# Attention's batch loops written out on five engines, and the last batch's outputs loaded first in the mixer

## What is computed

```python
x = x + _L0_xattn_ref(_layernorm(x), ctx_1024, Wq, bq, Wk, bk, Wv, bv, Wo, bo)
#  x (8, 128, 512), ctx_1024 (8, 2048, 512), 16 heads of 32
#  Q, K, V projected; scores = Q K^T / sqrt(32); weights = softmax(scores)
#  attn = weights V, joined over heads; attn @ Wo.T + bo
x = x + _L0_attn_ref(_layernorm(x), w_in, b_in, w_conv, b_conv, w_x, w_dt, A_log, D, w_out)
#  xr = x @ w_in + b_in (to 2048); xc, res = split(xr)
#  u = silu(causal_conv(xc)); x_dbl = u @ w_x; then the scan over positions
#  y * silu(res) @ w_out
x = x + _L0_ffn_ref(_layernorm(x), ...)
```

## Time and profile before

| | us |
|---|---|
| median of 3 runs | 2038.95 (2038.10 to 2041.55) |
| the profiled execution | 2038.54 |
| its span on the core | 2036.7 |
| mean granted TensorE clock | 0.985 |
| busy: TensorE, VectorE, GpSimd, ScalarE | 1937.5, 1423.7, 1261.3, 891.1 |
| attention's middle batches | 277 to 1070 in the span |
| attention ends, mixer_in begins | 1204.3 |
| mixer_in ends | 1318.0 |
| scan ends, experts begin | 1722.2 |

### The profile page before, as it was taken

How to read it: one execution, slowest core, us unless ns; L and a number is a source line. 1 busy time by engine, 2 the same in 40 slices (tenths; PEclk the granted TensorE clock), 3 DMA queues, 4 the chain that set the end, 5 groups by cost and what they waited for, 6 DMA issues and landing times. The chain is left out here.

```text
span 2036.7 us, 41293 instructions
## 1 busy us (share of the span) xinstructions
PE 1937.5 (95%) x15364; PEld 1417.2 (70%) x15364; DVE 1423.7 (70%) x1479; ACT 891.1 (44%) x1204; POOL 1261.3 (62%) x990
## 2 busy tenths in 40 slices
PE   6989999999999999999997879989999999999998
PEld 5867777777777777777774557655555555758886
DVE  4126777767676776776776845399999998538675
ACT  4124344333344343344433644376677664533340
POOL 4127777777677777777767731079998997325210
PEclk9999999999999999999997989999999999999999
DMA  5545565555555555556544320040040002111201
GB/s 187 162 139 176 155 190 164 176 176 167 170 167 173 167 176 155 183 156 189 163 139 148 116 65 0 24 104 1 1 115 10 1 1 94 46 44 62 86 19 42
DMA packets 180569, 229.56 MB, mean 113 GB/s; under 512 B 21489, under 2 KB 111921, under 8 KB 174225
## 3 DMA queue, kind: packets, MB, share of 16 engines
q1 hardware_dynamic: 180368, 226.82, 36.0%
HBM read 153.18 MB, written 73.56 MB: 111 GB/s over the span
## 5 line engine op out<-in xcount | busy, mean ns | idle before, releaser
L503 POOL TENSOR_TENSOR a_half<-a_pt 128x1024 f32<-128x1024 f32 x128 | 307.3, 2401 | 257.8 <-ACT a_pt L578 249.7
L578 ACT ACTIVATE a_pt<-a_shift 128x2048 f32<-128x2048 f32 x128 | 245.2, 1915 | 483.7 <-PE a_o L881 467.1
L683 DVE TENSOR_TENSOR a_shift<-a_s,a_neg_rows 128x2048 f32<-128x2048 f32 x113 | 258.9, 2291 | 92.1 <-ACT a_neg_rows L589 92.1
L670 DVE TENSOR_REDUCE a_top<-a_s 128x128 f32<-128x2048 f32 x113 | 259.0, 2292 | 52.3 <-PE a_s L838 50.6
L797 PE MATMUL a_pj<-l_x_hi,l_w_hi 128*128 128x512 f32 x448 | 208.6, 466 | 0.0
L494 POOL TENSOR_TENSOR l_x_lo<-a_raw,l_x_hi 128x512 fp32r<-128x512 f32 x120 | 155.6, 1297 | 80.3 <-ACT l_x_hi L565 80.3
L1270 POOL TENSOR_TENSOR s_even_drive<-s_du,l_rows 128x512 f32<-128x512 f32 x128 | 162.8, 1272 | 62.8 <-DMA s_c_row<-bc_scratch 60.1
L1278 POOL TENSOR_TENSOR s_odd_seen<-s_odd_state,s_c_row 128x512 f32<-128x512 f32 x128 | 162.4, 1269 | 34.3 <-DVE s_odd_state L1409 15.8
L1470 PEld LDWEIGHTS s_ps<-s_diag,s_du_t 128*128 128x128 f32 x1024 | 135.8, 194 | 62.0 <-issue 62.0
L799 PE MATMUL a_pj<-l_x_lo,l_w_hi 128*128 128x512 f32 x448 | 177.5, 396 | 0.0
L798 PE MATMUL a_pj<-l_x_hi,l_w_lo 128*128 128x512 f32 x448 | 177.4, 396 | 0.0
(11 more groups left out here) (268 smaller groups left out, 4053.9 us busy)
## 6 DMA issues: line engine op xcount, KB each, us to landing
kv_scratch<-a_k_new SPq DMA_DIRECT2D x128, 256.0 KB, 2.5
kv_scratch<-a_v_new SPq DMA_DIRECT2D x128, 256.0 KB, 3.2
a_stack<-kv_scratch SPq DMA_DIRECT2D x512, 64.0 KB, 2.3
a_v<-kv_scratch SPq DMA_DIRECT2D x32, 1024.0 KB, 5.6
a_raw<-in_ctx SPq DMA_DIRECT2D x120, 256.0 KB, 3.5
a_q_stack<-q_scratch SPq DMA_DIRECT2D x128, 64.0 KB, 2.6
s_c_row<-bc_scratch SPq DMA_DIRECT2D x32, 256.0 KB, 6.2
e_ew_raw<-in_ew SPq DMA_DIRECT2D x8, 1024.0 KB, 4.8
```

Source lines behind the costliest of these rows:

```text
L503: nc.gpsimd.tensor_tensor(half[:], w[:, 0:2], w[:, 2:4], ALU.add).then_inc(halved, 1)
L578: nc.scalar.activation(pt_head(g, p), shift[:].rearrange("p (i n) -> p i n", n=BANK), ACT.Exp).then_inc(exped, 1)
L670: dve.tensor_reduce(top[:], s_ps[:].rearrange("p i n -> p (i n)").rearrange("p (k q) -> p q k", q=L), AX.X, ALU.max).then_inc(blocked, 1)
L683: dve.tensor_tensor(shift[:].rearrange("p (k q) -> p k q", q=L), s_ps[:].rearrange("p i n -> p (i n)").rearrange("p (k q) -> p k q", q=L), ...
```

## The change

The five loops become loops of the program that writes the kernel, so all batches are straight code. In the last part of attention, `total` is split from `weigh`: everywhere but at the end it comes in the same place, and after the very last group it comes after the last transposes; VectorE takes one more row of norm steps (h = H + 2) before its last `finish_group`. In `mixer_in`, SP loads `b_in` alone, then waits for `a_stored` and loads `at`, then issues the other six loads; ScalarE waits for `b_in` and `at` (`a_in` 32) in place of all loads; TensorE transposes after tile 2 in place of tile 3 and makes tile 3 while the high and low parts are made; ScalarE empties tile 3 after that copy.

```diff
--- before.py
+++ after.py
@@ -446,7 +446,7 @@
                             store_out(b - 1, GROUPS - 1)
 
             heads(0, True, True, False)
-            with sp.Fori(1, B - 2) as b:
+            for b in range(1, B - 2):
                 heads(b, False, True, False)
             heads(B - 2, False, True, True)
 
@@ -531,7 +531,7 @@
                         add_weights(b, g, p, fresh)
 
             heads(0, True, True, False)
-            with pool.Fori(1, B - 2) as b:
+            for b in range(1, B - 2):
                 heads(b, False, True, False)
             heads(B - 2, False, True, True)
 
@@ -608,7 +608,7 @@
                             bias_keys(b + 1, g, p, p_ps[:, 0])
 
             heads(0, True, True, False)
-            with act.Fori(1, B - 2) as b:
+            for b in range(1, B - 2):
                 heads(b, False, True, False)
             heads(B - 2, False, True, True)
             def round_mixer_weights(n, k):
@@ -735,7 +735,7 @@
                         slot(b, g, p, first)
 
             heads(0, True)
-            with dve.Fori(1, B - 1) as b:
+            for b in range(1, B - 1):
                 heads(b, False)
             def add_output(j):
                 dve.wait_ge(ln.o_made, j + 1)
@@ -785,10 +785,10 @@
                     statistics(batch_at(h, 3))
                 if h % HG == HG - 1:
                     finish_group(*((B - 1, h // HG - 1) if h >= HG else (B - 2, GROUPS - 1)), True)
-            mixer_rows(H)
-            mixer_rows(H + 1)
+            for h in heads_and_after[H - 1:H + 2]:
+                mixer_rows(h)
             finish_group(B - 1, GROUPS - 1, True)
-            for h in heads_and_after[H + 1:]:
+            for h in heads_and_after[H + 2:]:
                 mixer_rows(h)
 
         @block.tensor
@@ -882,12 +882,14 @@
                                        pt_chunk(g, q, i)[:, j * L:(j + 1) * L], start=(i == 0 and j == 0),
                                        stop=(i == CH - 1 and j == KV - 1), tile_position=(0, DH * q))
                 mm.then_inc(weighed, 1)
-                if i == CH - 1:
-                    pe.wait_ge(parted, HG * (GROUPS * b + g + 1))
-                    for q in range(HG):
-                        mm = pe.matmul(o_ps[DH * q:DH * q + DH, L:2 * L], ones[:, :DH], part[:, g % 2, q],
-                                       start=True, stop=True, tile_position=(0, DH * q))
-                    mm.then_inc(totaled, 1)
+
+            def total(b, g):
+
+                pe.wait_ge(parted, HG * (GROUPS * b + g + 1))
+                for q in range(HG):
+                    mm = pe.matmul(o_ps[DH * q:DH * q + DH, L:2 * L], ones[:, :DH], part[:, g % 2, q],
+                                   start=True, stop=True, tile_position=(0, DH * q))
+                mm.then_inc(totaled, 1)
 
             pe.wait_ge(small_in, 32)
             pe.wait_ge(ones_out, 1)
@@ -903,6 +905,8 @@
                     weigh(b, g - 1, p, first)
                 elif not first:
                     weigh(b - 1, GROUPS - 1, p, False)
+                if p == CH - 1 and (g >= 1 or not first):
+                    total(*((b, g - 1) if g >= 1 else (b - 1, GROUPS - 1)))
 
             def slot(b, g, p, first):
                 h = HG * g + p
@@ -930,8 +934,9 @@
                         slot(b, g, p, first)
 
             heads(0, True)
-            with pe.Fori(1, B - 1) as b:
+            for b in range(1, B - 1):
                 heads(b, False)
+
             def project_output(h, lag, ks):
 
                 j = batch_at(h, lag)
@@ -979,6 +984,7 @@
                     turn_normalised(H + 1)
             for h in heads_and_after[H + 1:]:
                 turn_normalised(h)
+            total(B - 1, GROUPS - 1)
 
 
 DIN = 2 * D
@@ -1025,15 +1031,16 @@
 
         @block.sync
         def _(sp):
-            for dst, src in ((bi, b_in), (wc, w_conv), (bc, b_conv), (wx, w_x)) + to_load:
-                sp.dma_start(dst[:], src).then_inc(w_in_s, 16)
+            sp.dma_start(bi[:], b_in).then_inc(a_in, 16)
             sp.wait_ge(ln.a_stored, 16 * KC * B)
             sp.dma_start(at[:], a_scratch[J]).then_inc(a_in, 16)
+            for dst, src in ((wc, w_conv), (bc, b_conv), (wx, w_x)) + to_load:
+                sp.dma_start(dst[:], src).then_inc(w_in_s, 16)
             for s in range(2):
                 sp.dma_start(wi_raw[:, s], mix.w_in[:, :, mix.quarter(2 + s)]).then_inc(wi_in[s], 16)
             sp.wait_ge(xd_out, G)
             sp.dma_start(bc_scratch, xd[DTR:XD, :]).then_inc(a_in, 16)
-            sp.wait_ge(a_in, 32)
+            sp.wait_ge(a_in, 48)
 
         @block.gpsimd
         def _(pool):
@@ -1070,7 +1077,7 @@
                 nc.scalar.activation(u[:, c, :], acc[:, c % 2].rearrange("p b l -> p (b l)"), ACT.Silu,
                                      bias=bc[:, c:c + 1]).then_inc(u_done, 1)
 
-            act.wait_ge(w_in_s, 112)
+            act.wait_ge(a_in, 32)
             take_projected(0)
             act.wait_ge(ln.var_ready, J + 1)
             nc.scalar.activation(rstd[:], rstd[:], ACT.Sqrt).then_inc(ln.root_ready, 1)
@@ -1078,9 +1085,9 @@
             act.wait_ge(ln.scaled, J + 1)
             nc.scalar.activation(xn[:], xres[:, J, :], ACT.Identity, bias=shift_by[:], scale=rstd[:]).then_inc(ln.normed, 1)
             take_projected(2)
-            take_projected(3)
             act.wait_ge(ln.turned, J + 1)
             nc.scalar.copy(xn_hi[:, J], tp.rearrange("p (k l) -> p k l", k=KC)).then_inc(ln.hi_out, 1)
+            take_projected(3)
             for n in range(KC, len(tiles)):
                 if n == G * KC:
                     act.wait_ge(padded, 1)
@@ -1111,7 +1118,7 @@
             dve.wait_ge(ln.hi_out, J + 1)
             dve.tensor_tensor(xn_lo[:, J], tp.rearrange("p (k l) -> p k l", k=KC), xn_hi[:, J].bitcast(F32),
                               ALU.subtract).then_inc(ln.lo_out, 1)
-            dve.wait_ge(w_in_s, 112)
+            dve.wait_ge(w_in_s, 96)
             for c in range(DT):
                 dve.wait_ge(i_out, number[c, G - 1] + 1)
                 if c >= 2:
@@ -1131,7 +1138,7 @@
         @block.tensor
         def _(pe):
             def x_dbl():
-                pe.wait_ge(w_in_s, 112)
+                pe.wait_ge(w_in_s, 96)
                 pe.wait_ge(u_done, DT)
                 for g in range(G):
                     for c in range(DT):
@@ -1155,16 +1162,17 @@
                 mm.then_inc(i_made, 1)
 
             project(0)
-            pe.wait_ge(a_in, 16)
+            pe.wait_ge(a_in, 32)
             for k in range(KC):
                 mm = pe.matmul(op[:, 0, :], at[:, k, :], wo[:, k, :], start=(k == 0), stop=(k == KC - 1))
             mm.then_inc(ln.o_made, 1)
-            for n in range(1, KC):
+            for n in range(1, KC - 1):
                 project(n)
             pe.wait_ge(ln.normed, J + 1)
             for k in range(KC):
                 mm = pe.transpose(tp[:, k * L:(k + 1) * L], xn[:, k * P:(k + 1) * P], ident[:])
             mm.then_inc(ln.turned, 1)
+            project(KC - 1)
             pe.wait_ge(ln.lo_out, B)
             for n in range(KC, len(tiles)):
                 project(n)
```

## The result

The changed kernel ran in 2018.68 us (median of 4 runs, 2013.86 to 2019.66), the kernel before in 2038.53 in the same comparison: ratio 0.990, interval 0.988 to 0.992. The two intervals overlap. The profiled execution took 2017.81, its span is 2016.0, against 2038.54 and 2036.7. Where these 20.7 us of span went is the first question; why four runs could say 20 and six say 16 is the second.

A forecast was written before the change was run, and what follows sets the result against it. TensorE, busy 95% of the span, was taken to bound the kernel. Terms 10.0 + 3.7 + 1.7 + 1.5 = 16.9 us took 2038.54 to 2021.6; with 0.4 for the median, 2022.0 us was forecast, range 2019.0 to 2028.0.

The forecast's parts named there:

- rival 2: Attention's batch turns: branches are cheap and the stall comes from the turn itself; 7.4 us gain, 2031.6 us; chance 0.04.
- rival 3: TensorE's straight code outruns its instruction fetches, about 1.8 us per late one; slower, 2049 us with 15; chance 0.03.
- rival 1: Mixer start: last store lands late, so `at` is issued no earlier; 11.5 us gain, 2027.5 us; chance 0.10.
- The loops: Attention's five batches without TensorE's taken branches: 661.66 to 651.70 us, 10.0 us gained, bounds 8.5 to 10.4.
- The end of attention: Last batch's end: earlier transposes and low part of batch 5 let the mixer start 1.5 us earlier.
- Load order: Mixer start: `at` issued 4.2 us earlier, tile 0 next late; output product starts 3.7 us earlier, attention's 1.5 included.
- the seam's 1.5: Passage from attention to the mixer: 1.5 us earlier, counted inside the output product's 3.7 us.
- The 2.5 us that the range takes for it at worst: Worst-case share of the output product's earlier start, in the sum 8.5 + 2.5 + 0 + 1.0 = 12.0, 2026.5 us.
- Clock of the output product: Mixer's output product: without idle ahead, full clock, 3.1 us for 4.84; 1.7 us gained, bounds 0 and 1.7.
- Transposes: Mixer, a tile earlier: the wait for batch 7's low part goes, 1.54 us gained, lower bound 1.0.
- the stretches that the change leaves alone: Everything outside the edited loops, attention's end and mixer start: no term in the sum, so no gain claimed.
- best case: Whole kernel: 10.4 + 8.4, with tile 0 at full clock and `at` landing sooner, 18.8 us gained, 2019.7 us.

The follow-up runs named there:

- e4: The kernel before with the loops of SP, GpSimd, ScalarE and VectorE written out and TensorE's kept; ratio 0.9984 (0.9971 to 0.9998).
- e8: The kernel before with only the last batch's transposes moved ahead of tile 3; one execution, 2039.61 us.
- e1: The kernel before with only the five hardware loops written out on all engines; ratio 0.9962 (0.9944 to 0.9980).
- e6: The kernel before with only the order of the mixer's loads changed; one execution, 2032.77 us.
- e5: The changed kernel run again, unaltered, against the kernel before; 2020.79 us (6 runs), ratio 0.992 (0.990 to 0.994).

## Why the prediction was right or wrong

**Direction and places: right.** Every place named gave time, and no rival came: turns of 8.26 us (rival 2), no idle time inside the batches (rival 3), `at` issued 0.73 us after `b_in` (rival 1).

**The loops, 10.0 us, bounds 8.5 to 10.4: the place right, the bounds too narrow.** Against the one trace of before they gave 11.0 in the loops' stretch, since the straight batch takes 130.16 us and not the 130.34 I had built from a slot of 8.26 in place of 8.09 to 8.20. But as a price of the branches that trace was the dear end: its turns cost 9.8 to 10.1 us by the first scores, e4's second 9.39, and by VectorE's shifts the turns of the other five traces with TensorE's loop are 9.2 to 10.1, but for one at the low clock; and it held the low clock at a turn, which of the six such traces it and e8 have. By the traces of the experiments the loops cost 7 to 11 us, 9.0 by the means, and 7.7 by e1's runs. So 10.0 can stand and the bounds cannot. I took one execution's rows for a constant, a stretch at the low clock among them, and set the lower bound by taking off that stretch alone.

**The end of attention, 1.5 us: right**, 1.40; the store landed in time for the product, though `at` was issued 0.4 us later for it.

**Load order, 3.7 us with the seam's 1.5: right**, 1.4 and 2.4 make 3.8. The next thing late was tile 0, as said, 3.4 of its 4.4 us at half clock. The 2.5 us that the range takes for it at worst has no working.

**Clock of the output product, 1.7 us: right**, 1.8; e6 shows that the load order alone brings it. The traces with the old order vary, 4.7 to 6.1 us.

**Transposes, 1.54 us: right**, 1.66; they did not wait.

**The step that failed: the stretches that the change leaves alone.** The sum puts them at nothing, and the range gives them no width: its best case, 18.8 us, holds the named parts alone, and "the runs before lie up to 2.6 above their median" counted the spread on one side, without a look at what makes it. The runs showed 2.4 us there between the first two profiles, 0.8 of it in the tail of the last batch and 0.5 in the scan (402.7 us for 403.2). Without these 2.4 the profiled execution would have taken 2020.2 us and not 2017.8, inside the range; the rest of the miss is the loops' 11.0 for 10.0 and the other parts' 7.3 for 6.9. And they showed how wide such stretches are: the last batch alone takes 117.9 to 123.8 us with 27 to 41 us of low clock in it, and the 25 runs of before beside e1 range from 2030.53 to 2041.77. The first profile of the changed kernel had as little low clock in the last batch as that of before.

**The number.** 2022.0 was set against a median of 2038.95 from three runs; the later ones give 2036.9 to 2037.7. The same gain of 16.9 from there is about 2020.4, next to e5's 2020.79. So the sum came near the change partly by luck: its loops are 7 to 11 us by the trace that one takes, its seam and mixer 6.9 to 9.5 in place of 6.9, and I had drawn both from one trace. That the branches and not the turns, and the fetches behind them, cost the time was foreseen; that VectorE's 56 ns "agrees" with 108 holds for the order of size alone. Of the first four runs one (2013.86) had a mean clock of 0.989, which none of e5's six reached.

## What to carry to other kernels

A hardware loop whose body is long cost 4.3 to 5.1 us of TensorE's sequencer at each branch back here, with two fetches of code in it, and the array saw 1 to 2 us of that; one with a body of a single wait cost 0.2 us of the sequencer and nothing that could be seen in the time. Look for the closing branch by its line, and write out the loop of the engine that bounds the stretch. Before pricing from a trace, compare its granted clock with that of other executions: a stretch of 120 us in which TensorE waits in small gaps was 5 us longer or shorter by that alone. Matmuls that nobody reads, put into such gaps, held the clock and shortened that stretch by 4 to 9 us in a trace; in the runs they are shown to be worth it only together with the early loads.

## What was unexpected of the hardware

- The same program's last batch ran at a mean granted clock of 0.88 in one execution and 0.83 in another, 118.2 and 123.4 us; the cause of the choice between them is open.
- Extra matmuls in the waits, six in most heads, took the time at the low clock in that batch from 27 to 41 us down to 7, and to 3 with the early loads.
- A taken branch on TensorE took 4.3 to 5.1 us back over a batch and at most 0.23 us back over one wait, at the same places of the program; each of the 30 of the first kind had two instruction fetches in it, and none of the five of the second waited for one.
